# Attention over 8 batches on one core: the weighted values as fp32 products in two column halves of TensorE, with one copy per transposed block

## The chip, the cores and the metric

The kernel runs on one core of a Trainium2 chip. The metric is the device time of one launch in microseconds (us), the median of several runs. Durations of single instructions come from one profiled execution of the same program.

## What is computed

The input `x` is 8 sequences of 512 rows of 128 numbers, in fp32. Three residual blocks follow one another:

```
x = x + 0.5 * ffn(layernorm(x))     # 8 experts, the best 2 of a row, hidden size 512
x = x + attention(layernorm(x))
x = x + 0.5 * ffn(layernorm(x))

# attention: 16 heads of 64, ONE key and ONE value of 64 for all the heads
q = (x @ Wq) * 64**-0.5 ;  k, v = halves of (x @ Wkv)
sim  = q @ k.T + bias[bucket(i - j), head] * 8      # causal
attn = softmax(sim)
out  = (attn @ v for each head, heads side by side) @ Wout + bout
```

The change is in attention alone, in the step `attn @ v` and the product with `Wout` behind it.

## The kernel before, in words

Each engine runs its own instruction stream, tied to the others by semaphores. The three blocks run one after the other: `ffn_*(0)`, `attention(...)`, `ffn_*(1)`.

**Attention** goes batch by batch. A batch has 16 units `n`: 4 groups of 4 heads (`HG` = 4, `NG` = 4), times 4 tiles `t = n % 4` of 128 query rows. Unit `n` needs only the first `t + 1` blocks of 128 keys, so a group of heads has 1 + 2 + 3 + 4 = 10 blocks and a batch has 40. What follows happens for one unit:

- `S` (four times, one per head): TensorE multiplies `qst` by `kst` (L1039, L1040), VectorE adds the bias table and finds the row's extreme (L875), ScalarE takes the exponential with its row sum (L596).
- `R`: VectorE takes the reciprocal of the sums (L882), GpSimd scales `prob` of the unit, 4 heads at once (L526).
- `T` (once per block `jj`): TensorE transposes the 128x128 blocks of `prob` of the four heads into one bank (L1049). Then ScalarE copies the bank to `ph`, rounded to fp32r (L605), and VectorE subtracts that from the bank and writes the rest to `pl`, also fp32r (L887).
- `AV` (once per block): TensorE multiplies `vst` by `ph` (L1059) and by `pl` (L1061), 512 columns each (4 heads x 128 queries), and adds both in `OT_BANK`. `vst` holds the high part of the values in 64 columns and the low part in 64 more, so the bank has a high product on its partitions 0 to 63 and a low product on 64 to 127.
- `O`: ScalarE copies the bank to `ot` (L611).
- `Y`: TensorE multiplies each of the four heads of `ot` by the rows of `Wout` of that head (L1023). `wo_sb` holds these rows twice, on both halves of the partitions, so that the product also sums high and low parts. VectorE adds the result to `x_sb` (L865).

For each batch there are also `LN` (L841), `xT`, `K`, `V` and eight `Q` tasks: projections by three fp32r products each (`three`, L908 to L910), whose results ScalarE rounds (L585, L590) and VectorE subtracts from (L848, L853).

**Order.** No engine picks its work at run time. `attention_plan` gives each task a time in a unit of its own, `T` of block `jj` at `when`, `AV` at `when + LAG_AV` (2.0), `O` and `Y` behind the unit's last `AV`; tasks of the next batch are mixed in. `walk` sorts them by that time plus `LATER[(kind, engine)]`, and each engine's stream is written out in that order. A batch is one turn of the plan, so the plan's turn is run 8 times, with a start (`FIRST`) and an end (`FINAL`).

**Buffers.** Transposed blocks go through three banks (`PT_BANK`) and through `ph` and `pl` of `RING` = 3 slots each. Units take turns in two banks (`OT_BANK`), first for `AV` and then, over the same columns, for `Y`. Projections and scores take turns in three more banks (`FRONT_BANK`).

A transpose waits until the bank that it will write has been read (`pl_done` of block `i - 3`), and `ph` of a block waits for the `AV` of block `i - 3` (`av_ps`).

Of the kernel before, what the change touches and what calls it, by code (L numbers as in the profile page):

```python
# [9 lines left out]
P = 128  # L10
D = 128
# [11 lines left out]
RING = 3  # L23
# [20 lines left out]
LATER = {("S", "act"): 0.6, ("T", "dve"): 1.15, ("T", "act"): 0.5, ("Y", "dve"): 0.3, ("S", "dve"): 0.1,  # L44
         ("R", "dve"): 0.1, ("R", "pool"): 0.5, ("O", "act"): -0.25, ("xT", "act"): 0.3, ("K", "act"): 0.3,
# [33 lines left out]
def build(nc, x, Wq, Wkv, Wout, bout, rel_emb, gate_w, fc_w, proj_w, out):  # L79
    ctx = ExitStack()  # L80
    with ctx:
# [28 lines left out]
        wo_sb = sb("wo_sb", [P, H, D])  # L110
# [61 lines left out]
        with att:  # L172
# [7 lines left out]
            vst = ab("vst", [P, QT, 2 * DH], F32R)  # L180
# [39 lines left out]
        pt_ps, ph_done, pl_done, av_ps, bout_done, ot_done = (  # L220
            sem(n) for n in ("pt_ps", "ph_done", "pl_done", "av_ps", "bout_done", "ot_done"))
# [31 lines left out]
        def attention_plan():  # L253
# [49 lines left out]
        HIGHS = {"xT": 1, "K": 1, "V": 1, "Q": 2}  # L303
# [26 lines left out]
        def place_of(plan, b, task):  # L330

            m = tally(plan)[0][[x for _, x in plan].index(task)][0] + 1
            return m if plan is FIRST else b * NM + (PRE + m)
# [17 lines left out]
        def front_free(plan, b, task):  # L351
# [7 lines left out]
            if kind == "S":  # L359
                return s_done, (b + nb) * NS + (HG * rest[0] + rest[1] + 1)  # L360
            return misc_free, place_of(plan, b, (kind, nb, *rest))

        def attention(eng, run):
# [3 lines left out]
            run(FINAL, BATCH - 1)  # L367

# [62 lines left out]
        def _(gp):  # L431
# [20 lines left out]
            g.dma_start(rawkv, Wkv).then_inc(wa_in, 16)  # L452
            for z in range(2):
                g.dma_start(wo_sb[z * DH:(z + 1) * DH, :, :], Wout.rearrange("(h p) d -> p h d", p=DH)).then_inc(wa_in, 16)
# [79 lines left out]
        def _(act):  # L534
# [41 lines left out]
            def attention_act(plan, b):  # L576
                for task, m, hi in walk(plan, b, "act"):
# [3 lines left out]
                    if kind in ("xT", "K", "V"):  # L581
                        act.wait_ge(misc_ps, m + 1)
                        dst = {"xT": xTh[:], "K": kst[:, 0, :], "V": vst[:, :, 0:DH]}[kind]
# [503 lines left out]
```

## Time and profile before

| what | value |
|---|---|
| median of 3 runs | 1348.29 us (1348.22 to 1350.18) |
| the profiled execution's own time | 1350.1 us |
| its span, first to last instruction | 1348.4 us |
| attention, from the first `LN` to the last `Y` | about 332 us to 1050 us |
| one batch of attention, from one to the next | 88.5 us |
| TensorE busy over the span | 1086.5 us (81%) |
| VectorE, ScalarE, GpSimd busy | 67%, 57%, 48% |

A row of the trace names the line of the program, the engine (PE is TensorE, PEld its weight loads, DVE VectorE, ACT ScalarE, POOL GpSimd), the operation and the tiles as output<-inputs. Matmuls are pipelined and their ends are modelled: the record of one reaches beyond the start of the next. What one costs is the distance from its start to the next one's start. One fp32 matmul of the program shows as two records of each kind, one fp32r matmul as one.

### The profile page before, as it was taken

Reading aid. Unit: us, or ns where it says so; the run is one execution under the profiler, and the core shown is the slowest. Engines: PE = TensorE matmul, PEld = TensorE weight load, DVE = VectorE, ACT = ScalarE, POOL = GpSimd, SP = SyncE. Lnnn points to the kernel's source line nnn. Section 1 sums busy time; section 2 is a strip of 40 time slices with the busy share of each in tenths; the row PEclk is TensorE's granted clock in tenths of the full one; section 3 lists DMA queues with packets and bytes.
Section 4 is the critical chain, followed back from the end, with each engine's and each line's share of the span. In section 5 each row is a group of like instructions: output and inputs, shape, how many; then the busy total and the mean of one; then the engine's idle time right before and its main releaser. Section 6 shows DMA issues by size and latency. Waiting matters only on the chain.

```text
span 1348.4 us, 23234 instructions
## 1 busy us (share of the span) xinstructions
PE 1086.5 (81%) x6796; PEld 880.3 (65%) x6796; DVE 900.4 (67%) x2514; ACT 762.1 (57%) x1948; POOL 650.4 (48%) x473
## 2 busy tenths in 40 slices
PE   1419999960899999999999999999999707999990
PEld 1416676640787778878778778877787605677660
DVE  4663333337787888888888888888887394333336
ACT  1103333311888888888889889888898202333320
POOL 1146777743343444434444444444344044777763
PEclk9988999995999999999999999999999558999995
DMA  8892111131000000000000000000000201111115
GB/s 268 116 164 79 50 50 52 48 91 60 1 2 1 1 1 1 2 1 1 1 1 1 1 1 1 1 1 1 1 1 1 62 0 32 51 51 49 51 39 187
DMA packets 41366, 51.44 MB, mean 38 GB/s; under 512 B 5731, under 2 KB 30310, under 8 KB 41248
## 3 DMA queue, kind: packets, MB, share of 16 engines
q1 hardware_dynamic: 31504, 30.42, 9.3%
q0 software_dynamic: 9744, 19.56, 5.4%
q8 instruction: 61, 1.00, 0.3%
q14 instruction: 57, 0.47, 0.1%
HBM read 30.02 MB, written 20.97 MB: 38 GB/s over the span
## 4 chain that ended last, share of the span: by engine, by line
PE 50%; DVE 22%; POOL 10%; issue 9%; DMA 6%; ACT 1%; DVEq 1%; another core or an unknown queue 0%; SPq 0%; POOLq 0%; ACTq 0%
PE bank L1049 8%; PE bank L1023 6%; DVE qst L853 6%; POOL y_dram L494 6%; PE bank L1039 6%; PE bank L1040 5%; PE bank L1061 4%; PE bank L972 4%; PE bank L1059 4%; DMA xr<-xn_dram,gidx 4%; PE bank L989 3%; DVE prob L875 3%; POOL xr L488 3%; DVE x_sb L820 2%; DVE in_tile L749 2%
## 5 line engine op out<-in xcount | busy, mean ns | idle before, releaser
L526 POOL TENSOR_TENSOR prob<-prob,rsum 128x512 f32<-128x512 f32 (+3 forms) x128 | 296.0, 2321 | 381.1 <-DVE rsum L882 381.0
L596 ACT ACTIVATE prob<-prob,negmax 128x384 f32<-128x384 f32 (+3 forms) x512 | 283.1, 555 | 25.7 <-DVE negmax L875 24.1
L875 DVE CUSTOM_DVE_ANT_0 prob<-bank,bias_tab 128x384 f32<-128x384 f32 (+3 forms) x512 | 243.0, 490 | 69.6 <-PE bank L1040 59.4
L805 DVE COPY hT<-bank 128x512 f32<-128x512 f32 x144 | 99.6, 692 | 216.7 <-PE bank L980 216.4
L887 DVE TENSOR_TENSOR pl<-bank,ph 128x512 fp32r<-128x512 f32 x320 | 219.9, 687 | 26.1 <-ACT ph L605 22.4
L605 ACT ACTIVATE ph<-bank 128x512 fp32r<-128x512 f32 x320 | 189.1, 591 | 19.6 <-PE bank L1049 17.3
L1039 PE MATMUL bank<-kst,qst 128*128 128x256 f32 (+2 forms) x512 | 181.2, 368 | 23.5 <-DVE qst L853 21.1
L1049 PE MATMUL bank<-ident,prob 128*128 128x128 f32 x1280 | 193.5, 274 | 0.7 <-POOL prob L526 0.6
L1049 PEld LDWEIGHTS bank<-ident,prob 128*128 128x128 f32 x1280 | 156.8, 140 | 47.9 <-POOL prob L526 10.3
L488 POOL DMA_INDIRECT xr<-xn_dram,gidx x144 | 140.0, 973 | 73.3 <-issue 39.3
L494 POOL DMA_INDIRECT y_dram<-yo,sidx x144 | 146.1, 1014 | 60.2 <-issue 39.0
L568 ACT ACTIVATE xrT<-bank 128x128 f32<-128x128 f32 x144 | 40.0, 277 | 229.4 <-PE bank L965 229.3
L1040 PE MATMUL bank<-kst,qst 128*128 128x256 f32 (+2 forms) x512 | 160.0, 323 | 0.0
L972 PE MATMUL bank<-w_sb,xrT 128*128 x288 | 158.9, 634 | 0.0
L989 PE MATMUL bank<-w_sb,hT 128*128 x1152 | 153.2, 276 | 0.0
L574 ACT ACTIVATE hg<-bank 128x512 f32<-128x512 f32 x144 | 86.0, 597 | 102.6 <-PE bank L972 102.6
L1023 PE MATMUL bank<-wo_sb,ot 128*128 128x128 f32 x1024 | 141.1, 281 | 1.2 <-ACT ot L611 1.2
L989 PEld LDWEIGHTS bank<-w_sb,hT 128*128 128x128 f32 x1152 | 140.8, 193 | 0.3 <-issue 0.3
L1023 PEld LDWEIGHTS bank<-wo_sb,ot 128*128 128x128 f32 x1024 | 126.5, 191 | 20.1 <-ACT ot L611 17.3
L1059 PE MATMUL bank<-ph,vst 128*128 128x512 f32 x320 | 137.9, 431 | 0.0
L1061 PE MATMUL bank<-pl,vst 128*128 128x512 f32 x320 | 129.0, 403 | 4.9 <-DVE pl L887 4.9
L980 PEld LDWEIGHTS bank<-ident,hg 128*128 128x128 f32 x576 | 72.6, 142 | 76.5 <-issue 75.2
(155 smaller groups left out, 1589.8 us busy)
## 6 DMA issues: line engine op xcount, KB each, us to landing
in_tile<-y_dram SPq DMA_DIRECT2D x16, 512.0 KB, 4.2
bias_dram<-hg SPq DMA_DIRECT2D x1, 5120.0 KB, 52.9
xn_dram<-in_tile SPq DMA_DIRECT2D x8, 512.0 KB, 2.9
bias_tab<-bias_dram SPq DMA_DIRECT2D x1, 4096.0 KB, 13.4
xr<-xn_dram,gidx POOLq DMA_INDIRECT x144, 2.5
y_dram<-yo,sidx POOLq DMA_INDIRECT x144, 2.3
x_sb<-L_attn_x SPq DMA_DIRECT2D x4, 512.0 KB, 9.4
w_sb<-L_ffn_fc_w SPq DMA_DIRECT2D x1, 2048.0 KB, 17.9
```

The costliest lines, as they stand in the source:

```text
L494: g.indirect_dma_start(out=y2_dram[r], in_=yo[:, n % 4, :], in_offset=None, out_offset=bass.IndirectOffsetOnAxis(ap=sidx[:, n:n + 1], axis=0),
L526: g.tensor_tensor(out=pv, in0=pv, in1=rsum[:, n % 4, :].unsqueeze(2).to_broadcast([P, HG, (n % QT + 1) * P]), op=ALU.mult).then_inc(norm_d ...
L596: a.activation(prob[n % QT][:, h, :], prob[n % QT][:, h, :], ACT.Exp, scale=-1.0, bias=negmax[:, (HG * n + h) % 8:(HG * n + h) % 8 + 1], a ...
L875: v.tensor_tensor_reduce(out=prob[n % QT][:, h, :], in0=front[:, 0:w], in1=bias_tab[:, HG * (n // QT) + h, SEQ - w:SEQ], scale=-1.0, scala ...
L887: v.tensor_tensor(pl[:, i % RING, :], PT_BANK[i % 3][:], ph[:, i % RING, :].bitcast(F32), ALU.subtract).then_inc(pl_done, 1)
L972: t_.matmul(bank[2 + n % 2][:], xrT[:, n % 2, :], w1_sb[:, ds(e, 1), :].rearrange("p a f -> p (a f)"), start=True, stop=True).then_inc(up_ ...
L989: ins = t_.matmul(bank[6 + n % 2][:, 0:D], hT[:, n % 2, c * P:(c + 1) * P], w2_sb[:, ds(e, 1), c, :].rearrange("p a d -> p (a d)"), start= ...
L1023: ins = t_.matmul(OT_BANK[n % 2][:, 0:D], ot[:, n % 2, h * P:(h + 1) * P], wo_sb[:, HG * (n // QT) + h, :], start=(h == 0), stop=(h == HG ...
L1039: t_.matmul(front[:, 0:w], q, kst[:, 0, 0:w], start=True, stop=False)
L1040: t_.matmul(front[:, 0:w], q, kst[:, 1, 0:w], start=False, stop=True).then_inc(s_ps, 1)
L1049: ins = t_.transpose(PT_BANK[i % 3][:, h * P:(h + 1) * P], prob[n % QT][:, h, jj * P:(jj + 1) * P], ident[:])
L1059: t_.matmul(OT_BANK[n % 2][:], vst[:, jj, :], ph[:, i % RING, :], start=(jj == 0), stop=False)
```

## The change

- `vst` holds the values once, in fp32 (64 columns). The rounding and the subtraction for `V` become one copy on ScalarE, with a semaphore of its own (`v_done`).
- `ph` and `pl` become one fp32 ring `pT` of `RING` = 8 slots. A transposed block is copied once: blocks of even number by ScalarE, those of odd number by VectorE (`pt_done`, one semaphore for each).
- `AV` multiplies `vst` (128x64, fp32) by two heads at a time (256 columns in two runs of 128): heads 0 and 2 into partitions 0 to 63 of `OT_BANK`, heads 1 and 3 into 64 to 127. It is issued for up to `AV_BLOCKS` = 2 blocks at once.
- `O` copies 256 columns where it copied 512. `Y` is two matmuls over two heads each, 128 partitions deep, with `wo_sb` laid out to fit, into columns 256 to 383 of the bank.
- `O` and `Y` come later in the plan by 0.25 or 0.5; `LATER` changes for ("T", "dve") and ("O", "act"). `AV` of a batch's first two units now waits for `Y` of the batch before.

The diff, cut to its core:

```diff
-RING = 3
+RING = 8
+AV_BLOCKS = 2
-LATER = {("S", "act"): 0.6, ("T", "dve"): 1.15, ..., ("O", "act"): -0.25, ...
+LATER = {("S", "act"): 0.6, ("T", "dve"): 0.5, ..., ("O", "act"): 0.0, ...
...
-            vst = ab("vst", [P, QT, 2 * DH], F32R)
+            vst = ab("vst", [P, QT, DH])
-            ph = ab("ph", [P, RING, HG * P], F32R)
-            pl = ab("pl", [P, RING, HG * P], F32R)
-            ot = ab("ot", [P, 2, HG * P])
+            pT = ab("pT", [P, RING, HG * P])
+            ot = ab("ot", [P, 2, 2 * P])
...
-                    plan.append((when + LAG_AV, ("AV", n, jj)))
-                plan.append((when + LAG_AV + 0.01, ("O", n)))
-                plan.append((when + LAG_AV + LAG_Y, ("Y", n)))
+                    if jj % AV_BLOCKS == AV_BLOCKS - 1 or jj == t:
+                        first = jj // AV_BLOCKS * AV_BLOCKS
+                        plan.append((when + LAG_AV, ("AV", n, first, jj - first + 1)))
+                plan.append((when + LAG_AV + 0.25 * (t % AV_BLOCKS + 1), ("O", n)))
+                plan.append((when + LAG_AV + 0.25 * (t % AV_BLOCKS + 1) + LAG_Y, ("Y", n)))
...
+        def copied(i, engine):
+            return (i + 2 - engine) // 2
...
# ScalarE, T
-                        act.wait_ge(pt_ps, b * NB + (i + 1))
-                        if i >= RING:
-                            act.wait_ge(av_ps, b * NB + (i - RING + 1))
-                        a.activation(ph[:, i % RING, :], PT_BANK[i % 3][:], ACT.Copy).then_inc(ph_done, 1)
+                        if i % 2 == 0:
+                            act.wait_ge(pt_ps, b * NB + (i + 1))
+                            if i >= RING:
+                                act.wait_ge(av_ps, b * NB + (i - RING + 1))
+                            a.activation(pT[:, i % RING, :], PT_BANK[i % 3][:], ACT.Copy).then_inc(pt_done[0], 1)
# VectorE, T
-                        dve.wait_ge(ph_done, b * NB + (i + 1))
-                        v.tensor_tensor(pl[:, i % RING, :], PT_BANK[i % 3][:], ph[:, i % RING, :].bitcast(F32),
-                                        ALU.subtract).then_inc(pl_done, 1)
+                        if i % 2 == 1:
+                            dve.wait_ge(pt_ps, b * NB + (i + 1))
+                            if i >= RING:
+                                dve.wait_ge(av_ps, b * NB + (i - RING + 1))
+                            v.tensor_copy(pT[:, i % RING, :], PT_BANK[i % 3][:]).then_inc(pt_done[1], 1)
# TensorE, Y
-                        for h in range(HG):
-                            ins = t_.matmul(OT_BANK[n % 2][:, 0:D], ot[:, n % 2, h * P:(h + 1) * P], wo_sb[:, HG * (n // QT) + h, :],
-                                            start=(h == 0), stop=(h == HG - 1))
+                        for c in range(2):
+                            ins = t_.matmul(OT_BANK[n % 2][:, 2 * P:2 * P + D], ot[:, n % 2, c * P:(c + 1) * P], wo_sb[:, n // QT, c, :],
+                                            start=(c == 0), stop=(c == 1))
# TensorE, AV
-                        t_.matmul(OT_BANK[n % 2][:], vst[:, jj, :], ph[:, i % RING, :], start=(jj == 0), stop=False)
-                        pe.wait_ge(pl_done, b * NB + (i + 1))
-                        t_.matmul(OT_BANK[n % 2][:], vst[:, jj, :], pl[:, i % RING, :], start=False, stop=(jj == n % QT)).then_inc(av_ps, 1)
+                        for engine in range(2):
+                            if copied(last, engine):
+                                pe.wait_ge(pt_done[engine], b * (NB // 2) + copied(last, engine))
+                        if n == 0:
+                            pe.wait_ge(v_done, b + 1)
+                        if first == 0 and b * NU + n >= 2:
+                            pe.wait_ge(proj_done, b * NU + (n - 1))
+                        for jj in range(first, first + count):
+                            for o in range(2):
+                                heads = pT[:, blk(n, jj) % RING, :].rearrange("p (c o q) -> p o c q", c=2, o=2)[:, o, :, :]
+                                ins = t_.matmul(OT_BANK[n % 2][o * DH:(o + 1) * DH, 0:2 * P], vst[:, jj, :], heads,
+                                                start=(jj == 0), stop=(jj == n % QT))
+                            ins.then_inc(av_ps, 1)
```

## Rows read from the trace of the kernel before

**Rows 1.** The page: busy time of each engine, and the granted clock in 40 slices.
```profile
PE 1086.5 (81%) x6796; PEld 880.3 (65%) x6796; DVE 900.4 (67%) x2514; ACT 762.1 (57%) x1948; POOL 650.4 (48%) x473
PEclk9988999995999999999999999999999558999995
```

**Rows 2.** Busy time by stretch: one batch of attention, and six microseconds of the second ffn.
```profile
core 0: us, PE busy (x) PEld busy (x) DVE busy (x) ACT busy (x) POOL busy (x), PEclk, DMA share, GB/s
704.00:792.50 88.50, 82.93 (x540) 70.08 (x539) 74.56 (x227) 76.43 (x204) 38.29 (x17) 1.00 0.01 1
1179.00:1185.00 6.00, 5.74 (x39) 4.35 (x38) 2.88 (x6) 1.83 (x5) 4.78 (x5) 1.00 0.20 57
```

**Rows 3.** The tile vst: one subtraction a batch, durations, first and last start.
```profile
L848 DVE TENSOR_TENSOR vst<-bank,vst x8: 424/425/426, 350.1 to 969.3; 128x256 fp32r<-128x256 f32 x8
```

**Rows 4.** Waits in that batch, on TensorE: us in total, times, longest.
```profile
PE bank L1039 <- DVE qst L853: 2.7, 4, 0.8
PE bank L908 <- DVE qst L853: 1.9, 2, 1.0
PE bank L1061 <- DVE pl L887: 0.9, 3, 0.3
```

**Rows 5.** TensorE in order of time, in attention: start, us, what.
```profile
717.80 0.34 PE L1040 MATMUL bank<-kst,qst 128*128 128x384 f32 x1
717.97 0.40 PE L1059 MATMUL bank<-ph,vst 128*128 128x512 f32 x1
718.21 0.39 PE L1061 MATMUL bank<-pl,vst 128*128 128x512 f32 x1
718.44 0.60 PE L1049 MATMUL bank<-ident,prob 128*128 128x128 f32 x4
718.79 0.42 PE L1039 MATMUL bank<-kst,qst 128*128 128x384 f32 x1
719.05 0.34 PE L1040 MATMUL bank<-kst,qst 128*128 128x384 f32 x1
719.29 1.16 PE L1023 MATMUL bank<-wo_sb,ot 128*128 128x128 f32 x8
720.20 0.48 PE L1059 MATMUL bank<-ph,vst 128*128 128x512 f32 x1
...
726.69 1.10 PE L1023 MATMUL bank<-wo_sb,ot 128*128 128x128 f32 x8
727.55 0.48 PE L1059 MATMUL bank<-ph,vst 128*128 128x512 f32 x1
```

**Rows 6.** TensorE in order of time, in the second ffn.
```profile
1182.03 1.02 PE L972 MATMUL bank<-w_sb,xrT 128*128 x2
1182.89 0.60 PE L980 MATMUL bank<-ident,hg 128*128 128x128 f32 x4
```

**Rows 7.** Copies out of the banks, by shape: busy us, mean ns, idle before.
```profile
L887 DVE TENSOR_TENSOR pl<-bank,ph 128x512 fp32r<-128x512 f32 x40 | 27.5, 687 | 2.9 <-ACT ph L605 2.5
L605 ACT ACTIVATE ph<-bank 128x512 fp32r<-128x512 f32 x41 | 24.2, 591 | 2.2 <-PE bank L1049 1.8
L611 ACT ACTIVATE ot<-bank 128x512 f32<-128x512 f32 x16 | 9.5, 595 | 4.2 <-PE bank L1061 4.1
...
L805 DVE COPY hT<-bank 128x512 f32<-128x512 f32 x57 | 39.4, 692 | 81.5 <-PE bank L980 81.5
```

**Rows 8.** The tile vst again: ScalarE's rounding.
```profile
L585 ACT ACTIVATE vst<-bank x7: 384/384/384, 437.8 to 968.9; 128x256 fp32r<-128x256 f32 x7
```

**Rows 9.** The end of attention in order of time.
```profile
1046.87 0.69 DVE L887 TENSOR_TENSOR pl<-bank,ph 128x512 fp32r<-128x512 f32 x1 [0.23 <-ACT ph L605]
1047.61 0.50 PE L1061 MATMUL bank<-pl,vst 128*128 128x512 f32 x1 [0.18 <-DVE pl L887]
1048.15 0.60 ACT L611 ACTIVATE ot<-bank 128x512 f32<-128x512 f32 x1 [1.31 <-PE bank L1061]
1048.80 1.16 PE L1023 MATMUL bank<-wo_sb,ot 128*128 128x128 f32 x8 [0.69 <-ACT ot L611]
1049.99 0.29 DVE L865 TENSOR_TENSOR x_sb<-x_sb,bank 128x128 f32<-128x128 f32 x1 [2.43 <-PE bank L1023]
```

More of the change, by code:

```diff
@@ L109, in build @@
         wvs = sb("wvs", [P, 2, DH], F32R)
-        wo_sb = sb("wo_sb", [P, H, D])
+        wo_sb = sb("wo_sb", [P, NG, 2, D])
         bout_sb = sb("bout_sb", [P, D])
@@ L219, in build @@
                              "rsum_done", "norm_done"))
-        pt_ps, ph_done, pl_done, av_ps, bout_done, ot_done = (
-            sem(n) for n in ("pt_ps", "ph_done", "pl_done", "av_ps", "bout_done", "ot_done"))
+        pt_ps, av_ps, bout_done, ot_done, v_done = (sem(n) for n in ("pt_ps", "av_ps", "bout_done", "ot_done", "v_done"))
+        pt_done = [sem("pt_done_act"), sem("pt_done_dve")]
         block = ctx.enter_context(nc.Block())
@@ L330, in place_of @@
         def place_of(plan, b, task):
-            m = tally(plan)[0][[x for _, x in plan].index(task)][0] + 1
-            return m if plan is FIRST else b * NM + (PRE + m)
+            split = [x for _, x in plan if x[0] in USERS and x[0] != "V"]
+            m = split.index(task) + 1
+            return m if plan is FIRST else b * (NM - 1) + (PRE + m)
         FRONTS = 3
@@ L360, in front_free @@
                 return s_done, (b + nb) * NS + (HG * rest[0] + rest[1] + 1)
+            if kind == "V":
+                return v_done, b + nb + 1
             return misc_free, place_of(plan, b, (kind, nb, *rest))
@@ L452, in _ @@
             g.dma_start(rawkv, Wkv).then_inc(wa_in, 16)
+            wo_rows = Wout.rearrange("(c z p) d -> z p c d", z=2, p=DH)
             for z in range(2):
-                g.dma_start(wo_sb[z * DH:(z + 1) * DH, :, :], Wout.rearrange("(h p) d -> p h d", p=DH)).then_inc(wa_in, 16)
+                g.dma_start(wo_sb[z * DH:(z + 1) * DH, :, :, :].rearrange("p g c d -> p (g c) d"), wo_rows[z]).then_inc(wa_in, 16)
             g.dma_start(embT[:], rel_emb.rearrange("k h -> h k"), allow_slow_non_contiguous=True).then_inc(wa_in, 16)
@@ L842, in project_and_score @@
                                             mean[:, ds(t, 1)], rstd[:, ds(t, 1)], ALU.subtract, ALU.mult).then_inc(xa_done, 1)
[L843 removed]
+                    elif kind in ("xT", "K"):
                         dve.wait_ge(misc_hi, hi + 1)
[L845 to L848 removed]
+                        hi_t, dst = {"xT": (xTh[:], xTl[:]), "K": (kst[:, 0, :], kst[:, 1, :])}[kind]
+                        v.tensor_tensor(dst, front[:], hi_t.bitcast(F32), ALU.subtract).then_inc(misc_free, 1)
                     elif kind == "Q":
@@ L1051, in attention_pe @@
                     elif kind == "AV":
-                        _, n, jj = task
-                        i = blk(n, jj)
-                        pe.wait_ge(ph_done, b * NB + (i + 1))
-                        if n == 0 and jj == 0:
-                            pe.wait_ge(misc_free, place_of(plan, b, ("V", 0)))
-                        if jj == 0 and n >= 2:
-                            pe.wait_ge(proj_done, b * NU + (n - 1))
-                        t_.matmul(OT_BANK[n % 2][:], vst[:, jj, :], ph[:, i % RING, :], start=(jj == 0), stop=False)
-                        pe.wait_ge(pl_done, b * NB + (i + 1))
-                        t_.matmul(OT_BANK[n % 2][:], vst[:, jj, :], pl[:, i % RING, :], start=False, stop=(jj == n % QT)).then_inc(av_ps, 1)
+                        _, n, first, count = task
+                        last = blk(n, first + count - 1)
+                        for engine in range(2):
[4 more added lines that the diff above has]
+                        if first == 0 and b * NU + n >= 2:
+                            pe.wait_ge(proj_done, b * NU + (n - 1))
+                        for jj in range(first, first + count):
[4 more added lines that the diff above has]
+                            ins.then_inc(av_ps, 1)
             ffn_pe(0)
```

26 lines of the change are left out of this document (11 added, 15 removed).

## The prediction

> **What bounds the kernel now.** I read the page first, for the shares and the clock [rows 1], then the busy time by stretch [rows 2]. Over the whole span no engine is full. In attention, the only stage that the change touches, TensorE is busy 82.93 of 88.5 us, ScalarE 76.43, VectorE 74.56 and GpSimd 38.29, with the granted clock at 1.00, the level of 2.4 GHz. A batch takes (969.3 - 350.1) / 7 = 88.46 us [rows 3], so eight of them are 708 us of the span. The reader should see that TensorE sets this time, with two engines close behind it.
>
> Next the waits [rows 4]. TensorE idles 88.5 - 82.93 = 5.6 us a batch. Of that, 2.7 + 1.9 = 4.6 us in six gaps wait for VectorE's `qst`, and 0.9 us for `pl`. The six gaps are VectorE arriving late because it is 84% full.
>
> Last the timeline, for what a matmul really costs, from start to start [rows 5]. The fp32r product of 512 columns costs 0.23 to 0.24 us (717.97 to 718.21 to 718.44), though its record is 0.39 long. `Y`, four fp32 matmuls in 8 records, costs 0.91 and 0.86 us. The first fp32r matmul behind transposes costs 0.26 us where the same shape otherwise costs 0.17 (718.79 to 719.05; 717.80 to 717.97): 0.085 us, a price for changing the kind of matmul. An fp32 matmul of 512 columns in the ffn, at clock 1.00 [rows 2], costs 0.86 us in two records, 0.43 each [rows 6].
>
> **The change part by part,** for one batch (40 blocks, 16 units), as time on TensorE first.
>
> AV before: 40 x 2 x 0.2325 = 18.6 us. After, each block has two fp32 matmuls of 256 columns, hence four records. One record of 256 columns is half of one of 512: 0.215 us, an estimate from [rows 6]. What no row shows is whether the two column halves work at once, since every matmul of before has the full array (128*128). The bounds are four records in a row, 0.86 us a block, and both halves at once all through, 0.43 us. In between lies a staggered order: the records of one matmul (first and second pass) go to one half and cannot overlap each other, the next matmul goes to the other half, and TensorE starts matmuls in program order in all rows I saw. Then the second pass of one half runs with the first pass of the other. A group of two blocks takes 5 slots and one of a single block 3. `AV_BLOCKS` = 2 gives per group of heads four groups of two and two of one, so 16 and 8 a batch: 16 x 5 + 8 x 3 = 104 slots x 0.215 = 22.4 us. I take this middle value, as it needs the least beyond what the rows show. AV: +3.8 us (bounds -1.4 for 80 slots = 17.2 us, +15.8 for 160 slots = 34.4 us).
>
> Switches: 24 groups a batch enter the half-array form and leave it again, 48 switches. Nothing in the trace changes the array's form. The nearest row is the 0.085 us for a change of kind, and I take that: +4.1 us. Below lies nothing. Above lies a matmul's whole tail, 0.39 - 0.23 = 0.16 us [rows 5], plus a weight load that is no longer ahead, 0.50 - 0.39 = 0.11 us [rows 5, 9]: 0.27 us a switch, 13.0 us. The changes between fp32 and fp32r stay as many, as `AV` now stands between a score and a transpose.
>
> Y: 8 records become 4, and 0.86 becomes 0.43 us: 16 x 0.43 = -6.9 us. The new depth of 128 partitions is used before too.
>
> Copies: ScalarE loses 20 copies of 0.591 us and shortens 16 of 0.595 to the 0.384 of a 128x256 copy [rows 7, 8]: 76.4 - 11.8 - 3.4 = 61.2 us. VectorE loses 40 subtractions of 0.687, gains 20 copies of 0.692, the price of such a copy in the ffn, and loses one subtraction of 0.425 [rows 3, 7]: 74.6 - 27.5 + 13.8 - 0.4 = 60.5 us. None of it is on TensorE's path by itself, so I count nothing for it directly. It reaches TensorE through the idle time. Each of the six `qst` gaps stands behind a VectorE queue that held a `pl` of 0.69 us for every block and now holds one for every second. I take 0.4 us off each, 2.4 us, and the 0.9 us for `pl` goes: -3.3 us (bounds 0 and -5.6, all of the idle time). If this cover fails, the batch is 3.3 us longer than my sum.
>
> Waits: `AV` now waits for the copies of both its blocks, and behind it on TensorE are a transpose and scores. It is planned 2.0 plan units (88.46 / 42 = 2.1 us each) behind its last transpose, and one copy takes 0.7 us where two in a row took 1.3, so it should not stall. The ring of 8 slots frees copies earlier than 3 did. The wait of the first units for the last `Y` of the batch before is met a unit earlier. `Y` comes up to 0.5 plan units later and the next use of its bank a further unit later: nothing. GpSimd's stream and SP's queue are untouched in attention. `wo_sb` loads in two DMAs as before with half the bytes, in the first microseconds, under the first ffn: nothing. Two runs of 128 columns as moving operand: nothing, with the serial bound above it.
>
> The end: behind the last block a `pl` (0.69), half a `Y` (0.43) and the shorter `ot` (0.21) leave the chain [rows 9]: -1.3 us once.
>
> **Sum:** 3.8 + 4.1 - 6.9 - 3.3 = -2.3 us a batch, x 8 = -18.4, and -1.3 makes -19.7 us. The span goes from 1348.4 to 1328.7 us. The profiled run lasted 1350.1 us, 1.7 beyond its span, and the median of the runs, 1348.29, is lower by 1.8: taken off the median, the forecast is 1328.6 us.
>
> **The rivals.**
>
> *Both halves at once all through.* AV falls to 17.2 us, and -1.4 + 4.1 - 6.9 - 3.3 = -7.5 us a batch gives 1287 us. For it: the halves share neither weights nor output partitions. Against it: the second pass would have to let a later matmul past. The Trainium skill speaks for the weight of this rival: the page TensorE: Matmul & The Clock Gate, in Part 3 on packing small matmuls, has matmuls of different tiles start some 4 ns apart, and three column tiles gave 2.38 times the rate; the same part says that they start and end in program order, which is the stagger. No run here shows either yet.
>
> *No overlap.* 34.4 us: +15.8 + 4.1 - 6.9 - 3.3 = +9.7 us a batch, 1425 us. For it: no row shows two matmuls streaming at once. Against it: two outputs on separate partitions leave no dependence.
>
> *Dear switches, the one for slower with the mechanism of my forecast otherwise intact.* At each of the 48 places TensorE must empty before the array's form changes. The sum without switches is 3.8 - 6.9 - 3.3 = -6.4 us a batch, so it decides at 6.4 / 48 = 0.13 us a switch. At the tail alone, 0.16 us, the batch grows by 1.3 us and the time is 1357 us; at 0.27 us it grows by 6.6 us, 1400 us. For it: 0.085 us is already paid for a smaller change. Against it: the records' ends are modelled, so the tail may be shorter. The Trainium skill, on the page TensorEngine Tiling (Array Packing) under Key Properties, says that a change of the tiling mode drains the engine. By that rule the 0.16 us stands and the time is 1357 us, by the row it is 1328.6.
>
> *Idle time stays.* TensorE's written order leaves the six gaps where they are: 3.3 us a batch more than the forecast, 1355 us. This I take as the upper end of my forecast's own range, as both engines lose 14 to 15 us.
>
> **How the numbers follow.** Staggered with cheap switches 0.42, own range 1300 to 1355 us. Full overlap 0.25. Dear switches 0.16. No overlap 0.17. A run of this kernel can tell about 0.2%, 2.7 us, from no change. Full overlap is faster but for a dear switch, the forecast's case is faster in 0.34 of its 0.42: faster 0.60. Within 0.2% is a thin strip of two cases: 0.05. Slower: 0.35. The range goes from 1268 us, which leaves out 0.05 of the full overlap with free switches, to 1398 us, which leaves out the serial case at 1425 us and the very top of the dear switches, together 0.19 or so.
>
> **What the profile after would show.** Right: `AV` records of 128x256 whose starts lie 0.215 us apart within a half while the other half's lie on top of them, 1.1 us for a group of two blocks; 4 records a `Y` in 0.43 us; a first record behind the switch delayed by less than 0.1 us; `qst` waits of some 2 us a batch; ScalarE near 61 and VectorE near 60 us of a batch of 86.1 us. Wrong: a group of two that takes 1.72 us (serial) or 0.86 us (full overlap), gaps of 0.13 us or more at each switch, a batch whose idle time on TensorE has not fallen, or a clock under 1.00 in attention, on which every term rests.

## The result and the profile after

The changed kernel takes 1376.88 us (median of 4 runs) beside 1348.39 us for the kernel before: ratio 1.0205, 95% interval 1.0192 to 1.0218. It is 28 us slower. The forecast was 20 us faster, with 1268 to 1398 us as the range.

The page of the changed kernel, span and busy time of each engine (beside [rows 1]):

```profile
span 1376.4 us, 23194 instructions
PE 1072.7 (78%) x6924; PEld 795.0 (58%) x6924; DVE 791.7 (58%) x2346; ACT 663.4 (48%) x1788; POOL 650.0 (47%) x473
```

Every engine but GpSimd has clearly less to do than before, and the time is longer. So something waits. Busy time in one batch (beside [rows 2]), and the copy that marks each batch (beside [rows 3]), in the changed kernel:

```profile
704.00:796.30 92.30, 81.54 (x559) 59.13 (x555) 61.56 (x208) 64.20 (x183) 38.59 (x18) 1.00 0.01 1
```

```profile
L596 ACT ACTIVATE vst<-bank x8: 361/383/384, 347.6 to 993.5; 128x256 f32<-128x256 f32 x8
```

A batch takes (993.5 - 347.6) / 7 = 92.27 us instead of 88.46: +3.81, and eight times that is 30.5 us, the whole difference and 2 us more. In this batch the granted clock is 1.00, the level of 2.4 GHz. TensorE's busy time falls from 82.9 to 81.5 us, its idle time rises from 5.6 to 10.8.

Twice in attention, at 953 and at 1025 us, the clock falls for 3 to 4 us to 0.50, the level of 1.2 GHz, each time right behind a wait of TensorE of 1.75 us. The fence shows the wait, the `AV` behind it, and a microsecond by engines with the clock (0.50). This `AV` of two blocks takes 1.97 us where it else takes 1.08, and the batch with the first drop takes 93.6 us, the three ahead of it 92.0. So the drops are 0.2 of the 3.8 us, and the same wait stands in other batches with no drop behind it. Before the change attention has no drop.

```profile
952.89 0.36 PE L1051 MATMUL bank<-kst,qst 128*128 128x256 f32 x1 [1.75 <-DVE qst L863]
953.77 1.97 PE L1076 MATMUL bank<-pT,vst 128*64 128x256 f32 x8
956.00:957.00 1.00, 1.00 (x6) 1.00 (x5) 0.00 (x0) 0.00 (x0) 1.00 (x1) 0.50 0.00 0
```

What `AV` costs is seen in TensorE's order of time, changed kernel (beside [rows 5]; the second fence is the start of the group at 735.01 in a view cut off at 735.3 us):

```profile
731.98 0.34 PE L1052 MATMUL bank<-kst,qst 128*128 128x384 f32 x1
732.25 0.65 PE L1076 MATMUL bank<-pT,vst 128*64 128x256 f32 x4
732.83 0.66 PE L1061 MATMUL bank<-ident,prob 128*128 128x128 f32 x4
...
734.74 0.34 PE L1052 MATMUL bank<-kst,qst 128*128 128x384 f32 x1
735.01 1.08 PE L1076 MATMUL bank<-pT,vst 128*64 128x256 f32 x8
736.03 0.66 PE L1061 MATMUL bank<-ident,prob 128*128 128x128 f32 x4
```

```profile
735.01 0.65 PE L1076 MATMUL bank<-pT,vst 128*64 128x256 f32 x4
```

A record of this shape lasts 0.38 us, so the fourth starts 0.65 - 0.38 = 0.27 us behind the first, and the eighth 0.70. Four records in a row, 0.215 us each (a slot), would put the fourth at 0.65, and the staggered order of the prediction at 0.43. They start in pairs instead, the two of a pair within 0.01 us: a block takes two slots, a group of two takes four. The group of one costs 0.58 us from start to start, the group of two 1.02. Two slots make 0.43 and four 0.86: 0.15 to 0.16 us is left. Of it about 0.095 lies behind the last pair and 0.05 behind the first. The entry costs 0.27 - 0.17 = 0.10 more (731.98 to 732.25). The transpose behind an `AV` takes 0.41 us to the next start (732.83 to 733.24), one that does not stand behind an `AV` 0.36.

Where TensorE waits, in 600 us of attention (6.5 batches) of the changed kernel; the columns are us in total, times, longest:

```profile
PE bank L1051 <- DVE qst L863: 36.9, 26, 1.8
PE bank L920 <- DVE qst L863: 12.7, 13, 1.3
PE bank L1076 <- DVE pT L900: 6.9, 13, 0.6
PE bank L920 <- DVE xTl L858: 6.1, 6, 1.3
```

The same stretch of the kernel before, whose single batch is in [rows 4]:

```profile
PE bank L1039 <- DVE qst L853: 19.2, 28, 0.8
PE bank L908 <- DVE qst L853: 13.4, 14, 1.0
PE bank L1061 <- DVE pl L887: 4.2, 14, 0.3
```

The wait of the first score for `qst` doubled. It stands at four places of the plan in each batch (26 times in the stretch). TensorE at the first of them, before and then after the change:

```profile
707.99 0.50 PE L908 MATMUL bank<-xTh,wqs 128*128 128x512 f32 x1 [0.97 <-DVE qst L853]
709.25 1.05 PE L1023 MATMUL bank<-wo_sb,ot 128*128 128x128 f32 x8
710.06 0.48 PE L1059 MATMUL bank<-ph,vst 128*128 128x512 f32 x1
710.61 0.60 PE L1049 MATMUL bank<-ident,prob 128*128 128x128 f32 x4
711.85 0.35 PE L1039 MATMUL bank<-kst,qst 128*128 128x256 f32 x1 [0.64 <-DVE qst L853]
```

```profile
721.44 0.50 PE L920 MATMUL bank<-xTh,wqs 128*128 128x512 f32 x1 [1.30 <-DVE qst L863]
722.71 0.60 PE L1061 MATMUL bank<-ident,prob 128*128 128x128 f32 x4
723.14 0.61 PE L1035 MATMUL bank<-wo_sb,ot 128*128 128x128 f32 x4
725.30 0.36 PE L1051 MATMUL bank<-kst,qst 128*128 128x256 f32 x1 [1.55 <-DVE qst L863]
726.18 1.08 PE L1076 MATMUL bank<-pT,vst 128*64 128x256 f32 x8
```

From the second Q to the first score that needs it: 711.85 - 707.99 = 3.86 us before, 725.30 - 721.44 = 3.86 us after. Here the chain Q, rounding on ScalarE, subtraction on VectorE, score has not become a hundredth shorter. Inside it lay a `Y` of 0.81 us, an `AV` of 0.55 and a transpose; now lie a transpose and a `Y` of half the length, and the `AV` pair stands behind the scores at 726.18. What was saved here gives nothing: its place is a wait. The moved part, which cost nothing here, is now paid outside.

At the four places of a batch the distance was 3.86, 3.91, 3.91 and 3.26 us, with waits of 0.64, 0.64, 0.64 and 0.82. It is 3.86, 4.79, 4.79 and 3.27 now, with waits of 1.55, 1.75, 1.75 and 0.56. So at two places the chain even grew, by 0.88 us. The second of the four places, after the change (Q starts at 742.09):

```profile
742.89 0.61 PE L1035 MATMUL bank<-wo_sb,ot 128*128 128x128 f32 x4
743.51 0.50 PE L1051 MATMUL bank<-kst,qst 128*128 128x512 f32 x1
744.41 0.69 DVE L885 CUSTOM_DVE_ANT_0 prob<-bank,bias_tab 128x512 f32<-128x512 f32 x1 [0.95 <-PE bank L1052]
745.03 0.28 DVE L875 TENSOR_TENSOR x_sb<-x_sb,bank 128x128 f32<-128x128 f32 x1
745.34 1.39 DVE L863 SCALAR_TENSOR_TENSOR qst<-bank,qst 64x512 fp32r<-64x512 f32 x2
746.88 0.36 PE L1051 MATMUL bank<-kst,qst 128*128 128x256 f32 x1 [1.75 <-DVE qst L863]
```

VectorE's written order has the bias of one more score ahead of the subtraction for `qst`, so it waits for that score. Before, the score came right behind Q (729.24, with Q at 728.45); now the later `Y` stands between them (742.89), and its sum into `x_sb` stands ahead of the subtraction too.

### The profile page after: what moved, and what is told of

The parts are those of the page before. It is cut to its first block, busy times and chain, and to the rows that moved or that the text cites. A ratio compares the mean times of both kernels' runs of the same rounds, so it can differ in the third digit from the quotient of the medians.

```text
span 1376.4 us, 23194 instructions
## 1 busy us (share of the span) xinstructions
PE 1072.7 (78%) x6924; PEld 795.0 (58%) x6924; DVE 791.7 (58%) x2346; ACT 663.4 (48%) x1788; POOL 650.0 (47%) x473
## 3 DMA queue, kind: packets, MB, share of 16 engines
q8 instruction: 62, 1.02, 0.3%
## 4 chain that ended last, share of the span: by engine, by line
PE 45%; DVE 20%; POOL 14%; issue 11%; DMA 6%; ACT 1%; DVEq 1%; another core or an unknown queue 0%; SPq 0%; POOLq 0%; ACTq 0%
PE bank L1061 8%; PE bank L1076 8%; POOL prob L536 6%; PE bank L1051 5%; POOL y_dram L504 5%; DMA xr<-xn_dram,gidx 5%; PE bank L1052 5%; DVE qst L863 4%; PE bank L984 4%; POOL xr L498 3%; PE bank L1001 3%; PE bank L1035 2%; DVE prob L885 2%; DVE x_sb L832 2%; DVE in_tile L761 2%
## 5 line engine op out<-in xcount | busy, mean ns | idle before, releaser
L1051 PE MATMUL bank<-kst,qst 128*128 128x256 f32 (+2 forms) x512 | 187.5, 378 | 46.7 <-DVE qst L863 44.3
L1061 PE MATMUL bank<-ident,prob 128*128 128x128 f32 x1280 | 203.3, 282 | 5.9 <-POOL prob L536 5.0
L1061 PEld LDWEIGHTS bank<-ident,prob 128*128 128x128 f32 x1280 | 143.6, 141 | 89.5 <-issue 23.8
L1076 PE MATMUL bank<-pT,vst 128*64 128x256 f32 x1280 | 182.2, 397 | 12.0 <-DVE pT L900 8.5
L504 POOL DMA_INDIRECT y_dram<-yo,sidx x144 | 146.1, 1014 | 61.2 <-issue 36.4
L1052 PE MATMUL bank<-kst,qst 128*128 128x256 f32 (+2 forms) x512 | 162.4, 326 | 0.0
L1051 PEld LDWEIGHTS bank<-kst,qst 128*128 128x128 f32 x512 | 98.2, 192 | 60.6 <-issue 44.3
L900 DVE COPY pT<-bank 128x512 f32<-128x512 f32 x160 | 109.8, 686 | 25.6 <-PE bank L1061 23.8
L1076 PEld LDWEIGHTS bank<-pT,vst 128*64 128x64 f32 x1280 | 78.1, 137 | 75.2 <-issue 40.1
L617 ACT ACTIVATE pT<-bank 128x512 f32<-128x512 f32 x160 | 93.9, 587 | 32.0 <-PE bank L1061 28.8
L1052 PEld LDWEIGHTS bank<-kst,qst 128*128 128x128 f32 x512 | 99.1, 194 | 1.3
```

What stands on the lines that cost most here:

```text
L504: g.indirect_dma_start(out=y2_dram[r], in_=yo[:, n % 4, :], in_offset=None, out_offset=bass.IndirectOffsetOnAxis(ap=sidx[:, n:n + 1], axis=0),
L900: v.tensor_copy(pT[:, i % RING, :], PT_BANK[i % 3][:]).then_inc(pt_done[1], 1)
L1051: t_.matmul(front[:, 0:w], q, kst[:, 0, 0:w], start=True, stop=False)
L1052: t_.matmul(front[:, 0:w], q, kst[:, 1, 0:w], start=False, stop=True).then_inc(s_ps, 1)
L1061: ins = t_.transpose(PT_BANK[i % 3][:, h * P:(h + 1) * P], prob[n % QT][:, h, jj * P:(jj + 1) * P], ident[:])
L1076: ins = t_.matmul(OT_BANK[n % 2][o * DH:(o + 1) * DH, 0:2 * P], vst[:, jj, :], heads, start=(jj == 0), stop=(jj == n % QT))
```

## The experiments

All are one-line or few-line edits. "Batch" is (last - first start of the copy or rounding into `vst`) / 7. The kernel before took 1348.9 to 1349.6 us beside them, except for e9, e10 and e11, which ran on another chip where it took 1428.56 us. In the traces of these three the first `vst` comes at 385 to 389 us instead of 346 to 350, and behind the last one the run is 40 us or more longer; a record of `AV` in attention lasts 0.379 us as in the other runs. So for these three the batch is compared. No trace of the kernel before exists from that chip; by the ratios e11 costs 3.0 us a batch over the changed kernel, by the batches 3.3.

| run | time, us | ratio to before (95%) | batch, us |
|---|---|---|---|
| before | 1348.39 | | 88.46 |
| after | 1376.88 | 1.0205 (1.0192 to 1.0218) | 92.27 |
| e1 copy behind qst | 1385.40 | 1.0260 (1.0243 to 1.0277) | 93.76 |
| e2 one block | 1387.94 | 1.0281 (1.0264 to 1.0298) | 93.70 |
| e3 before, half Y | 1327.65 | 0.9834 (0.9818 to 0.9851) | 85.69 |
| e4 early Q | 1335.78 | 0.9899 (0.9882 to 0.9915) | 87.23 |
| e5 before, early Q | 1364.34 | 1.0102 (1.0080 to 1.0124) | 90.23 |
| e6 same half | 1445.97 | 1.0716 (1.0690 to 1.0743) | 100.93 |
| e7 wide Q | 1335.38 | 0.9892 (0.9871 to 0.9912) | 87.41 |
| e8 Q first | 1341.50 | 0.9944 (0.9925 to 0.9963) | 88.01 |
| e9 early AV | 1559.50 | 1.0931 (1.0905 to 1.0958) | 105.47 |
| e10 early Q and AV | 1483.63 | 1.0377 (1.0343 to 1.0411) | 96.17 |
| e11 full Y | 1480.91 | 1.0381 (1.0358 to 1.0405) | 95.59 |
| e12 split second | 1386.95 | 1.0285 (1.0262 to 1.0309) | 93.60 |
| e13 Y soon | 1368.28 | 1.0141 (1.0118 to 1.0163) | 91.19 |
| e14 copies soon | 1322.55 | 0.9804 (0.9782 to 0.9825) | 85.71 |
| e15 split, Y soon | 1368.81 | 1.0145 (1.0128 to 1.0162) | 91.27 |
| e16 before, same order | 1396.62 | 1.0352 (1.0335 to 1.0369) | 94.77 |
| e17 copies soon, Y 0.25 | 1345.21 | 0.9969 (0.9959 to 0.9979) | 88.41 |

A drop of the clock behind a wait also stands in the batches of e1, e6, e9, e10 and e16. Batches with no drop take 92.4 us in e1, 100.0 in e6, 95.2 in e10, 93.8 in e16 and 92.0 in the changed kernel; e9 has at least one in every batch. The other runs have none in the seven batches.

### Do the halves run at once? (e6)

Of all blocks but a unit's first, both products go to the lower half, so the output of heads 1 and 3 is wrong in part.

```diff
-  ins = t_.matmul(OT_BANK[n % 2][o * DH:(o + 1) * DH, 0:2 * P], vst[:, jj, :], heads,
+  z = o if jj == 0 else 0
+  ins = t_.matmul(OT_BANK[n % 2][z * DH:(z + 1) * DH, 0:2 * P], vst[:, jj, :], heads,
...                                    # the flag `stop` is set to fit
```

> The kernel after in which AV of all blocks but a unit's first (24 of 40 a batch) sends both products to the lower half of the array and of the partitions; the output of heads 1 and 3 is then wrong in part. Theory (the two halves run at once, and only because they are different halves): records of one block 0.215 us apart where pairs started together, 24 x 0.43 = 10.3 us more on TensorE a batch, of which a fifth lies in waits: 1376.9 + 8 x 8 = about 1441 us, at most 1460. Rival (what starts together in the trace is only how records are drawn): the time stays within 10 us of 1377.

The batch grew by 8.7 us (8.0 between batches with no drop of the clock), of 10.3 put on TensorE. A group of two blocks, the first in both halves and the second in one:

```profile
735.53 1.51 PE L1077 MATMUL bank<-pT,vst 128*64 128x256 f32 x8
```

The eighth record starts 1.51 - 0.38 = 1.13 us behind the first instead of 0.70: two slots more for one block. So the overlap is real, and it comes from the two halves. The length of a group alone could not have told: 1.02 us is near the 1.1 us that the prediction named for the staggered order. The run also shows that work outside the gaps counts for the most part.

### Is work at the chain free? (e3, e11)

e3 leaves out half of the output projection; e11 makes each product of it twice.

```diff
# e3, the kernel before, Y
-    for h in range(HG):
+    for h in range(2):
...
# e11, the kernel after, Y
-    for c in range(2):
+    for h in range(HG):
+        c = h % 2
...
```

> The kernel before with Y over two of the four heads: it leaves out half of the output projection, 6.9 us of TensorE a batch. Rival (TensorE's work sets the batch, as the prediction had it): 1348.3 - 8 x 6.9 = 1293 us. Theory (where TensorE waits for the qst chain, its work is only cover): what lies between a Q and the first score gives nothing back; of 16 Y a batch some 4 to 6 lie there or in front of the Q behind another Q, so 40 to 70 per cent of the 55 us come back, 1310 to 1326 us, with longer waits for qst.

> The kernel after with four matmuls in Y as before, each of the two products made twice (so the attention output is doubled): it puts the 6.9 us of TensorE a batch back that the change took from Y, and leaves the order as it is. Theory (a good part of Y lay in waits): Y stands directly in front of four of the gaps a batch and near two more, and there 0.43 us costs nothing: +3.5 to +5 us a batch, 1405 to 1417 us. Rival (the batch is set by the chain alone): within 10 us of 1377. Rival (TensorE's work sets it): 1376.9 + 55 = 1432 us.

Halving `Y` in the kernel before gave 2.8 us a batch of the 6.9 taken away, and its waits for `qst` in front of scores rose:

```profile
PE bank L1039 <- DVE qst L853: 31.0, 42, 1.1
```

31.0 us in 600 where it was 19.2. At the first of the four places the distance stayed, 3.85 us, and the wait grew from 0.64 to 1.08: half a `Y` of 0.43 us gave nothing there. Putting the other half back in the changed kernel cost 3.3 us a batch of 6.9 put on. More than half of `Y` was covered by waits either way: this is the term -6.9 of the forecast, worth 2.8 to 3.3. The expectations had the right kind of answer and were a little off in size: e3 came at 1327.65 us (1310 to 1326 expected), e11 at +3.3 us (+3.5 to +5).

### Is it the chain behind Q? (e4, e7, e8, e14)

```diff
-Q_AT = -2.1
+Q_AT = -2.9                     # e4, e7, e8, e14
-Q_GAP = 1.1
+Q_GAP = 1.5                     # e7, e14
# of the table LATER, the other entries cut:
-  ("Q", "act"): 0.3, ("Q", "dve"): 0.9
+  ("Q", "act"): 0.0, ("Q", "dve"): 0.7          # e8
-  ("T", "dve"): 0.5, ("T", "act"): 0.5
+  ("T", "dve"): 0.2, ("T", "act"): 0.2          # e14
```

> The kernel after with Q_AT = -2.9 for -2.1: both Q of groups 1 to 3 are issued 0.8 plan units (1.7 us) earlier, so that 1.7 us more of other work lies between the second Q and the first score that needs it. Theory (the batch is set by the chain behind Q): the wait of about 1.5 us in front of the first score of three groups goes, 3 x 1.5 = 4.5 us a batch, about 1341 us; the wait of the second Q for the first stays. Rival (the waits are a symptom, the time is set by another loop, GpSimd's scaling or the copies): gaps move elsewhere and the time stays above 1368 us.

> The kernel after with Q_AT = -2.9 and Q_GAP = 1.5: the first Q as early as in the run with early Q, the second 0.4 plan units (0.9 us) later. Theory: the second Q waits 0.9 us less for the bank of the first (2.1 us in two waits a batch now), while the first score is 0.9 us nearer to the second Q and waits 0.4 us more in three groups: between -1.0 and +0.5 us a batch, 1328 to 1340 us. Rival (another loop sets the time already): within 2 us of 1335.8.

> The kernel after with Q_AT = -2.9 and LATER of (Q, act) 0.0 for 0.3 and of (Q, dve) 0.7 for 0.9, so that ScalarE takes qst in front of an exponential that waits for VectorE. Theory (latency of the chain behind Q is what counts): the chain gets shorter by up to 0.7 us, the two waits of the second Q shrink from 2.1 us to under 1: 1328 to 1334 us. Rival (the exponentials delayed by it hold up scaling and transposes): 1336 us or more.

> The kernel after with Q_AT = -2.9, Q_GAP = 1.5 and LATER of (T, dve) and (T, act) 0.2 for 0.5. With Q early, transposes that wait for a bank to be copied are 1.4 us of a batch and AV that wait 1.7 us. Theory (with the gaps at Q gone, the next limit is the copies out of the three banks): 0.5 to 1.5 us a batch less than with Q_GAP = 1.5 alone, 1323 to 1331 us. Rival (copies then stand in front of qst and of the scores, and block VectorE while the transpose runs): 1336 us or more.

With both Q of three of the four groups of heads 1.7 us earlier in the plan (e4) and nothing else, 41 us go. The wait in front of the first score, in the run with early Q:

```profile
PE bank L1051 <- DVE qst L863: 5.6, 14, 0.6
```

5.6 us where the changed kernel has 36.9. The order of the plan, not the matmuls, held the time. The wide Q (e7) moved waits and won nothing. Taking Q in front of the exponentials on ScalarE (e8) lost 0.8 us a batch, as its rival had it, and `Y` then waited for `ot` (10.9 us in the stretch, none of note in e4). With the wide Q and the copies sooner (e14) the batch is 85.71 us and the kernel 2.0% faster than the one before (1322.55 us, where 1323 to 1331 was expected); waits for `pT` are gone from the list:

```profile
PE bank L920 <- DVE qst L863: 10.7, 7, 1.5
PE bank L1051 <- DVE qst L863: 8.3, 14, 0.9
PE bank L920 <- DVE xTl L858: 7.0, 7, 1.3
PE bank L1035 <- ACT ot L623: 6.5, 14, 0.7
```

### Is that order good for the kernel before too? (e5, e16)

The same edits in the kernel before; e16 with `Q_GAP` = 1.5 and both copies 0.3 sooner.

> The kernel before with the same Q_AT = -2.9 that made the changed kernel 41 us faster. Theory (in the kernel before, longer matmuls hid most of the chain behind Q, so there is less to win; 2.7 us a batch wait for qst in front of a score): -1 to -2.5 us a batch, 1328 to 1341 us, about level with the changed kernel with early Q. Rival (the change itself is worth what the forecast said once both have their Q early): the kernel before stays at 1345 to 1350 us.

> The kernel before with the order that made the changed kernel fastest: Q_AT = -2.9, Q_GAP = 1.5, copies 0.3 sooner on both engines (0.85 and 0.2). Theory (ScalarE and VectorE are 86 and 84 per cent full there, so an order that leans on their free time gives nothing): 1348 to 1370 us. Rival (the order is better for either kernel): below 1340 us.

No. It made the kernel before slower by 1.0% and 3.5%; the theory's own figure for e5, a gain of 8 to 20 us, was wrong in sign, and e16 came 27 us above the upper end of its theory. Some 6 us of that are drops of the clock (a batch with one takes 94.7 us, one with none 93.8). In e16 TensorE waits more for `qst` than with its own order:

```profile
PE bank L1039 <- DVE qst L853: 30.9, 25, 1.6
PE bank L908 <- DVE qst L853: 14.7, 7, 2.1
```

So this order suits the one kernel and not the other; no further order was tried for the kernel before. That it can't use an earlier Q because ScalarE and VectorE are full fits the numbers (86 and 84%, [rows 2]) but was not tried alone.

### What opened the gap? (e1, e2, e9, e10, e12, e13, e15, e17)

Parts of the change were undone, one by one and together: where VectorE's copy stands (e1), pairs (e2, e12), the pair's time (e9, e10), the later `O` and `Y` (e13, e17), the last two together (e15).

```diff
# the changed values alone, all else cut
-("T", "dve"): 0.5
+("T", "dve"): 1.15                       # e1
-AV_BLOCKS = 2
+AV_BLOCKS = 1                            # e2
-LAG_AV = 2.0
+LAG_AV = 1.2                             # e9; e10 with Q as in e7
+pair = 1 if t == 1 else AV_BLOCKS        # e12, e15
-0.25 * (t % AV_BLOCKS + 1)
+0.01                                     # e13, e15
-0.25 * (t % AV_BLOCKS + 1)
+0.25                                     # e17, on e14
```

> The kernel after with LATER of (T, dve) back at 1.15, so that VectorE takes its copy of a transposed block behind the subtraction for qst and not in front of it; nothing else changes. Theory (the batch is set by the chain Q on TensorE, qst on ScalarE, qst on VectorE, next matmul, and the copy of 0.69 us now stands in it): where the copy stands in front, one qst a group of heads comes 0.6 us earlier, some 2.4 us a batch, so 1376.9 - 19 = about 1358 us, and the gaps before the Q matmul behind the first Q shrink from 1.3 to about 0.7 us. Rival (only the lost cover on TensorE matters): the time stays within 3 us of 1377, since the gap in front of the first score, 1.55 us, has no copy in its chain.

> The kernel after with AV_BLOCKS = 1: AV is issued block by block, so one AV stands again in the stretch in which TensorE waits for qst, and O and Y come 0.25 units behind. 40 groups a batch for 24. Theory of lost cover: 4 AV of 0.6 us go back into waits, -2.4 us a batch, against 16 more entries and exits of 0.19 to 0.24 us each, +3 to +3.8 us, of which some lie in waits too: 1377 to 1388 us. Rival (switches and not waits made the change slow): each group more costs its full 0.24 us and nothing comes back, 1376.9 + 8 x 3.8 = 1407 us. Rival (pairing is what made it slow): below 1360 us.

> The kernel after with LAG_AV = 1.2 for 2.0 plan units. In the kernel before, AV of the first block of the second tile lay between the second Q and the first score that waits for it; issued in a pair, it comes a unit later, behind that score. With 1.2 the pair is planned just in front of the score again. Theory (the gap grew because its cover was moved away): some 1.2 us of AV go back into each of the gaps in front of a first score, the waits of 5.6 us a batch fall to about 2, and with O and Y earlier too the batch takes 3 to 4 us less: 1345 to 1353 us. Rival (the chain for the copies is now too short, and AV waits for pT instead): 1370 us or more.

> The kernel after with Q_AT = -2.9, Q_GAP = 1.5 and LAG_AV = 1.2 together. Theory: both remedies fill the same gap, so they do not add; 0 to 1 us a batch better than 1335.4: 1327 to 1336 us. Rival (AV waits for its copies where it comes so early): 1338 us or more.

> The kernel after in which the two blocks of the second tile of a group are issued singly, as before the change, and the rest in pairs: AV of the first of them stands again between the second Q and the first score. 28 groups a batch for 24. Theory (the AV moved out of the gap is part of what was lost): four gaps of 1.55 us get some 0.6 us of cover each, -2.4 us a batch, four more groups cost 4 x 0.24 = +1.0 us: some -1 to -1.5 us a batch in all, 1365 to 1370 us, with the wait of the first scores down from 5.6 to about 3.5 us. Rival (only the halved Y and the copy in front of qst opened the gap): 1377 to 1385 us.

> The kernel after with O and Y of a unit planned 0.01 behind its last AV, as before the change, and not 0.25 or 0.5. Theory: the offset only leaves room for ScalarE's copy; Y of the first tile stays ahead of the first score either way: 1374 to 1382 us. Rival (the offset is what moved work across the gap): under 1368 us.

> The kernel after with the second tile's blocks issued singly and O and Y planned 0.01 behind the last AV: the plan's order around the first scores is that of the kernel before. In the run with the split alone the gap in front of the first score shrank, but AV then waited for the sum of an earlier Y into x_sb (23 us over 6.8 batches, none of note in the kernel after). Theory (moved AV and late Y together opened the gap): the wait for x_sb goes, some 3 us a batch, and the gap stays small: 93.6 to about 90 us a batch, 1350 to 1362 us. Rival (the chain behind Q has its length whatever lies in it, and what is filled here opens there): 1365 us or more.

> The fastest order so far (Q_AT = -2.9, Q_GAP = 1.5, copies at 0.2) with O and Y 0.25 behind the last AV for every unit, for 0.25 and 0.5. Theory: Y waits for ot 1.1 us a batch already and would wait 0.3 us more, while bank and x_sb are free sooner: 1320 to 1326 us, no change that can be told. Rival (as in the run with Y soon, where 0.24 to 0.49 units less gave 1.1 us a batch): 1313 to 1318 us.

e1 did at its place what was expected (the gap of 1.31 us fell to 0.70, the waits of the Q matmuls for `qst` from 12.7 to 4.9 us in the stretch) and lost as much elsewhere:

```profile
PE bank L1051 <- DVE qst L863: 37.3, 27, 1.8
PE bank L1076 <- DVE pT L900: 13.1, 12, 1.1
PE bank L920 <- DVE xTl L858: 6.0, 6, 1.3
PE bank L920 <- DVE qst L863: 4.9, 7, 0.7
PE bank L1076 <- ACT pT L617: 4.4, 6, 0.7
```

`AV` now waited for its copies, 13.1 + 4.4 us where it was 6.9. Between batches with no drop of the clock that makes 0.4 us (92.4 beside 92.0). The rest of the 1.5 us by which the mean batch is longer is the clock: it fell six times in the seven batches, each time right behind a wait of 1.75 us in front of a first score, and a batch with two drops takes 95.4 us, so one costs 1.5. Without the drops e1 would lie near 1380 us, an estimate from 0.4 us a batch, which is nearer the rival's 1377 than the theory's 1358. e2 landed at the upper end of the theory: first scores waited 19.7 us, not 36.9, the waits of Q matmuls for `qst` rose to 18.0, and 16 more groups a batch cost more than was gained. e9 and e10 missed by far, 105 and 96 us a batch: moving every `AV`, `O` and `Y` 1.7 us earlier made `AV` wait for copies (25.7 us in e9), and the waits for `qst` rose (46.0). With longer waits the clock fell more often: from 440 to 1000 us its mean is 0.95 in e9 and 0.98 in e10, and 1.00 in the changed kernel. By some 20 such drops in the seven batches of e9 at 1.5 us each, an estimate from e1, the clock is 4 of its 13 us a batch over the changed kernel. In e12, whose time lies above both of its ranges, the gap closed and opened next door:

```profile
PE bank L1077 <- DVE x_sb L876: 23.0, 19, 1.2
PE bank L921 <- DVE qst L864: 12.7, 13, 1.3
PE bank L1062 <- POOL prob L537: 12.7, 20, 0.9
PE bank L1052 <- DVE qst L864: 9.1, 13, 0.8
```

The single `AV` needs the bank that an earlier `Y` still holds, as `O` and `Y` are planned later now. e13 alone gave 1.1 us a batch, outside both of its expected ranges: the two distances of 4.79 us went back to 4.14. e15 removed the wait for `x_sb` as expected, and still took 91.27 us, no less than e13; transposes waited for GpSimd's scaling instead (13.6 us, 4.4 in the changed kernel). Its theory, that moved `AV` and late `Y` together opened the gap, falls; its rival holds. e17 shows the sharpness of the order: `Y` of every second unit 0.25 plan units (0.5 us) earlier cost 2.7 us a batch of the fastest order, where no change was expected, and the rival expected a gain.

## Why the prediction was wrong

**The stage and the bound.** Right that only attention changes, and nearly right that the clock stays: its drops are 0.2 us a batch. Wrong in taking TensorE's work as what sets the batch. The prediction read 82.9 us busy of 88.5 as the bound and the six `qst` gaps as VectorE arriving late because it is full. The gaps are the visible ends of a chain of 3.3 to 3.9 us, most of which lay under matmuls.

**AV, +3.8 us.** The pick between the three orders was wrong and the full overlap right: 80 slots, 17.2 us, so -1.4 by slots. The Trainium skill's page TensorE: Matmul & The Clock Gate, Part 3 on packing small matmuls, has matmuls of different tiles start nearly together, and here eight records start in four pairs (first to fourth 0.27 us); no record shows which pass a pair holds.

**Switches, +4.1 us.** Right in kind, and too small: about 0.10 us at the entry and 0.095 at the exit, and 0.05 behind the first pair, 0.24 a group, 5.8 us a batch. The rival's 0.16 us did not come. The Trainium skill's page TensorEngine Tiling (Array Packing), Key Properties, says that a change of mode drains the engine; the trace shows a cost at both changes, smaller than the tail of 0.16 us. AV and switches together: forecast +7.9 us. Added up from start to start over one batch, gaps of 0.2 us and more taken out, `AV` takes 21.2 us both before and after (before, one behind a `Y` took 0.32 us and not 0.23), scores take 23.8 and then 26.1, for the entry falls on them, and transposes 16.0 and then 17.5: +3.8.

**Y, -6.9 us.** Nearly right as work (4 records in 0.36 to 0.47 us where nothing else is waited for; -5.7 a batch from start to start), wrong as time: e3 and e11 show 2.8 to 3.3 us.

**Copies.** VectorE 61.6 us a batch, forecast 60.5; ScalarE 64.2, forecast 61.2. The copies last 0.685 and 0.587 us, `ot` 0.376, all near the forecast. ScalarE's records overlap: by groups they add up to 91.3 us before and 75.3 after, so a record less takes less than its length from the busy time.

**Idle, -3.3 us: the step that failed.** The prediction let the shorter queue of VectorE take 0.4 us off each of six gaps. In one batch with the clock at 1.00 TensorE's gaps grow from 5.6 to 10.5 us, +4.9 where -3.3 was forecast: an error of 8.2 us a batch, 66 us in all. TensorE's work, added up as above, falls from 82.9 to 81.5 us, -1.4 where 3.8 + 4.1 - 6.9 = +1.0 was forecast, and makes 2.4 of it good. 4.9 - 1.4 = 3.5, and the drops of the clock bring the mean to 3.8. Of the 4.9 us, 2.9 are the four first scores. That the gaps stand behind a `pl` for every block, and now behind a copy for every second, was wrong in place: `LATER` put the copy in front of the `qst` of the first Q (its chain, 707.99 - 703.88 = 4.1 us before, became 721.44 - 716.74 = 4.7, and e1, with the copy behind, has 4.1 again), and the `pl` had stood behind it. In front of the first scores shown above, the subtraction stands behind the bias of a score that VectorE still waits for, and one copy less does not bring that score forward.

**Waits and order, counted at nothing.** "`Y` comes later: nothing" was wrong by 1.1 us a batch (e13): at two places it put a `Y` into the chain behind Q and lengthened it by 0.88 us. That pairs move an `AV` across a score was not looked at in the plan.

**The rivals.** "Idle time stays" had the right place and too small a price: it let the gaps stay, not grow. A rival in which work leaves a covered place was missing, and the plan's own constants showed where. Of the forecast for the profile after, full overlap and unshrunk idle time were named as signs of error, and both came. The result lies 48 us above the forecast and still in the range of 1268 to 1398 us, but that is luck: dear switches filled the upper part of the range, and they did not come.

**What stays open.** How the 3.8 us divide among the edits. `Y` later is 1.1 us and the drops of the clock 0.2; the rest is not one edit. Each of e1, e2 and e12, which undo one alone, was slower (e1 by 0.4 us a batch without its drops of the clock), and what one filled opened at the next chain, copies, `x_sb` or GpSimd's scaling. That the order as a whole is the cause is shown by e4 and e14, which change nothing but the plan. Why the clock falls behind some waits of 1.75 us and not behind others is open.

## What to carry to other kernels

In an order written by hand, an engine that is 94% busy can still not be the bound: measure from the instruction that starts a chain to the one that waits for its end, and see what lies under it. If that distance is fixed, work taken from under it is worth nothing until the chain starts earlier. Look at every place of the plan: here two of four kept their distance and two grew. Read the clock of each run before explaining its waits. A change that alters lengths needs its own order before it is judged: the same matmuls were 2.1% slower with one plan and 2.0% faster with another, and that other plan made the kernel before 3.5% slower.

## What the runs showed of the hardware

- Two fp32 matmuls (128x64 weights, 256 columns) in the two column halves run fully at once at clock 1.00: a block of four records takes two slots of 0.215 us. Sent to one half, it takes four (e6).
- Going from the full array to a half costs about 0.10 us, back about 0.095, and the first pair 0.05 more. The transpose behind it takes 0.41 us from start to start and not 0.36.
- The granted clock fell for 3 to 4 us to the level of 1.2 GHz behind waits of 1.75 us with TensorE busy before and after (two times in the changed kernel's attention, six in seven batches of e1), at 1.5 to 1.6 us of a batch each. Waits of the same length in the same trace had no drop behind them.
- Another chip ran the same kernel before in 1428.56 us instead of 1349. Traces of other variants from it have the same record of `AV`, 0.379 us, and lose 76 to 89 us outside the seven batches; where exactly was not followed.
